# A TensorE bank lent for one decay, the attention norm by tokens, and a shifted split between VectorE and GpSimd in a state-space and attention kernel

## The chip, the cores and the metric

One core of one Trainium2 chip runs the whole kernel. The metric is the time of one execution on the device in microseconds (us). The page and the trace show one profiled execution; the times of the table come from runs of their own. Engines: PE is TensorE (PEld its weight loads), DVE VectorE, ACT ScalarE, POOL GpSimd, SP the engine on whose queue all DMAs of the loop are issued.

## The reference, cut to what matters

The input x is (8, 96, 64, 64): eight batches, 96 channels, 4096 positions ("tokens"). Everything is fp32 but the last block.

```python
# layer 0: group norm, then a selective state-space block
xz = u @ in_proj_w.T;  xm, z = halves of 192 channels
xm = silu(causal depthwise conv of 4 taps(xm) + conv_b)
dt, Bm, Cm = xm @ x_proj_w.T          # 6, 16, 16 columns
delta = softplus(dt @ dt_proj_w.T + dt_proj_b)
h_t = exp(delta_t * A) * h_(t-1) + delta_t * B_t * u_t   # 192 channels x 16 states
y_t = C_t . h_t + D * u_t
out = layernorm_c((y * silu(z)) @ out_proj_w.T) * gamma + beta
x = x + out
# layer 1: linear attention (no softmax) of 6 heads on t = tokens of x
t = t + ((q k^T / 4) v) @ Wff + bff    with q, k, v from layernorm(t) @ Wqkv + bqkv
# then a feed-forward 96 -> 384 -> 96 in 8-bit products on layernorm(t)
t = t + ffn(layernorm(t))
```

Since the attention has no softmax, it needs of a batch only the 97x97 Gram matrix of the normed tokens with a row of ones ("G" below): four small products ("fold") turn G into a matrix that is applied to every token.

## The kernel before, in words

**Tiling.** A batch is cut into 8 chunks of T = 512 positions; 64 chunks are worked one after the other. The states of a chunk are laid out as 24 blocks of 128 rows, 6 "quads" (s) of 4 blocks (q): quads 0 to 3 hold the lower 128 channels (LOWS), quads 4 and 5 the upper 64 (HIGHS).

**Per block.** ACT computes the decay exp(delta*A) of a block into one of two PSUM banks DA (decay, L834); DVE scans it, h = decay*h + D, into R (scan, L1271). D, the product of delta*u and B, has room for three quads: DVE forms it for quads 0 and 1 and for the first SPLIT = 240 columns of quad 3 (inputs, L1255; its B stands in the PSUM bank PB, copied there by ACT: put_b, L820), POOL for quads 2, 4 and 5 (inputs, L648) and the rest of quad 3 (rest, L657). POOL also multiplies R by C, one instruction per quad (product, L669), and forms delta*u (delta_u, L641). PE sums the products over the states (sum_states, L1639 and L1643) into the bank Y, and DVE gates them with silu(z) (gate, L1292).

**Around it.** In iteration g the block work is that of chunk g. PE and ACT prepare chunk g+1 (silu L782 to L789 with a table load before and after, x_proj, state_rows L796, dt_proj, softplus) and g+2 (norm L773, conv L1596 and L1599, z_proj). They finish chunk g-1 (out_proj, square L840, variance, inv_ln L845, inv_std L849, scale_out L1296, add_x, keep_x1 L882, centre) and the attention's part of g-2: DVE's token_norm (L1304) makes th, the normed x1; PE transposes it (to_tokens L1700), ACT copies it to tT (token_copy L877), PE forms four products of 128 tokens (gram L1709) and DVE adds them to G (L1330). Chunks g-10 to g-12, a batch later, go through attention and the feed-forward (centre_tokens L1751, variance_x2, inv_ln_x2 L892, norm_x2 L1351, up, hidden L901, down, output L923, x2 sums, result L916).

**Order.** Every engine has one queue with its order written out by hand in its function iteration(g). Waits are on semaphores; the names Progress hold a count per chunk. The four general PSUM banks G0 to G3 pass from use to use, each guarded by what last read it (freed in PE's iteration). SP's queue is one order too: a DMA that waits holds all behind it. B, C, delta and delta*u are spread over the 128 rows through DRAM: spill writes them, spread_delta, spread_du, load_b and load_c read them back (L487, L489, L509, L515). keep_th (L440) stores th.

## Time and profile before

| | |
|---|---|
| median of 3 runs | 2515.29 us (2514.42 to 2517.96) |
| profiled execution | 2515.68 us, its span 2513.9 us |
| mean granted TensorE clock in it | 0.986 |
| DVE, POOL, ACT, PE busy | 98%, 96%, 92%, 85% of the span |
| DMA | 494.54 MB, mean 197 GB/s |

The span runs from the first instruction to the last; 1.8 us lie around it. A busy share is that of the whole span, with its start (60 us) and its end (some 100 us), in which other work is done than in the loop. Busy time counts an instruction from its start to its end; neighbours on one engine overlap by 0.05 to 0.1 us, so that the distance of two starts is what an instruction costs.

### The profile page before, as it was taken

What the parts mean: (1) busy time and instruction counts of PE and PEld (TensorE: products, weight loads), DVE (VectorE), ACT (ScalarE), POOL (GpSimd) and SP (SyncE); (2) the same over time, 40 slices, a digit from 0 to 9 for tenths busy, and PEclk for the clock granted to TensorE, in tenths of its full rate; (3) what the DMA queues carried; (4) which work ended last, traced back from release to release, by engine and by line L of the source; (5) the groups of instructions that cost most, each with busy time, mean ns of one, the idle gap of its engine ahead of it and who ended that gap; (6) DMA issues with size and microseconds to landing.
All of it is one profiled execution on the core that took longest, in us unless ns stands there. A gap on an engine that the chain in (4) does not pass through costs nothing.

```text
span 2513.9 us, 35083 instructions
## 1 busy us (share of the span) xinstructions
PE 2145.8 (85%) x10314; PEld 827.2 (33%) x10314; DVE 2456.3 (98%) x2391; ACT 2316.1 (92%) x3960; POOL 2418.5 (96%) x719
## 2 busy tenths in 40 slices
PE   6888888888888888888888888888888888888878
PEld 3334434333323323323333323323323333333323
DVE  6999999999999999999999999999999999999986
ACT  5777777999999999999999999999999999999977
POOL 4999999999999999999999999999999999999991
PEclk8899999999999999999999999999999999999979
DMA  6555555656656656656656666566566565566542
GB/s 240 192 184 167 199 185 175 210 197 199 217 197 205 211 198 205 210 203 203 207 203 206 204 207 209 198 209 210 196 210 209 197 209 201 189 211 199 183 141 75
DMA packets 171388, 494.54 MB, mean 197 GB/s; under 512 B 23072, under 2 KB 44704, under 8 KB 154240
## 3 DMA queue, kind: packets, MB, share of 16 engines
q1 hardware_dynamic: 171200, 492.30, 58.2%
q8 instruction: 85, 1.39, 0.2%
q14 instruction: 103, 0.84, 0.1%
HBM read 400.33 MB, written 91.88 MB: 196 GB/s over the span
## 4 chain that ended last, share of the span: by engine, by line
DVE 66%; POOL 14%; issue 12%; PE 3%; ACT 3%; DMA 0%; DVEq 0%; POOLq 0%; ACTq 0%; SPq 0%
DVE R L1271 50%; POOL R L669 10%; DVE D L1255 10%; POOL D L648 3%; DVE q L1351 1%; ACT DA L834 1%; DVE dl L1281 1%; DVE G L1296 1%; DVE yv L1292 1%; PE G L1562 1%; POOL D L657 1%; DVE th L1304 1%; POOL du L641 1%; PE Y L1643 1%; PE Y L1562 0%
## 5 line engine op out<-in xcount | busy, mean ns | idle before, releaser
L1271 DVE TENSOR_TENSOR_SCAN R<-DA,R,D 128x512 f32<-128x512 f32 x1344 | 1633.6, 1270 | 1.0 <-ACT DA L834 1.0
L669 POOL TENSOR_TENSOR R<-R,Cs 128x2048 f32<-128x2048 f32 x383 | 1453.8, 3821 | 0.0
L834 ACT ACTIVATE DA<-ds,kept_w 128x512 f32<-128x512 f32 x1536 | 1054.9, 688 | 143.4 <-DVE R L1271 129.4
L648 POOL TENSOR_TENSOR D<-us,Bs 128x2048 f32<-128x2048 f32 x193 | 738.0, 3824 | 9.8 <-DMA us<-lo_d 9.8
L1255 DVE TENSOR_TENSOR D<-us,PB 128x2048 f32<-128x2048 f32 x191 | 360.3, 1886 | 7.2 <-DMA us<-lo_d 7.2
L1596 PE MATMUL G<-un,wcv 96*128 96x512 f32 x512 | 251.7, 614 | 29.4 <-ACT h L901 29.4
L1639 PE MATMUL Y<-R,kept_w 128*32 128x512 f32 x2048 | 265.3, 613 | 8.3 <-POOL R L669 8.3
L1271 DVE TENSOR_TENSOR_SCAN R<-DA,D 128x512 f32<-128x512 f32 x192 | 221.9, 1206 | 2.1 <-ACT DA L834 2.1
L1599 PE MATMUL G<-un,wcv 96*64 96x256 f32 x1024 | 138.9, 393 | 60.5 <-ACT xq L882 59.2
L1562 PE MATMUL G<-st,kept_w 128*64 128x256 f32 (+1 forms) x384 | 108.9, 485 | 54.3 <-ACT st L796 54.3
L1596 PEld LDWEIGHTS G<-un,wcv 96*128 96x128 f32 x512 | 87.9, 189 | 187.8 <-issue 113.8
L1562 PE MATMUL G<-sq,kept_w 96*96 96x512 f32 (+1 forms) x256 | 136.7, 616 | 13.2 <-DVE dl L1281 12.6
L1643 PE MATMUL Y<-R,kept_w 128*32 128x256 f32 x2048 | 138.1, 388 | 7.7 <-POOL R L669 7.6
L657 POOL TENSOR_TENSOR D<-us,Bs 128x1088 f32<-128x1088 f32 x64 | 135.7, 2121 | 4.4 <-DVE R L1271 4.0
L1562 PE MATMUL G<-q,w1q 96*128 96x512 fp8e5 x164 | 63.1, 388 | 77.7 <-DVE q L1351 45.4
L905 ACT ACTIVATE h<-h,b1q 128x512 f16<-128x512 f16 x165 | 117.2, 711 | 0.0
L1599 PEld LDWEIGHTS G<-un,wcv 96*64 96x64 f32 x1024 | 62.6, 136 | 148.3 <-ACT xq L882 111.3
L1562 PE MATMUL G<-un,kept_w 96*64 96x256 f32 x372 | 108.1, 470 | 0.0
L1639 PEld LDWEIGHTS Y<-R,kept_w 128*32 128x32 f32 x2048 | 47.6, 110 | 162.3 <-issue 106.3
L641 POOL TENSOR_TENSOR du<-dl,u 128x768 f32<-128x768 f32 x63 | 97.9, 1554 | 0.0
L820 ACT COPY PB<-Bs 128x512 f32<-128x512 f32 x191 | 95.6, 500 | 0.0
L901 ACT CAST h<-G 128x512 f16<-128x512 f32 x164 | 94.8, 578 | 0.3 <-PE G L1562 0.3
(239 smaller groups left out, 3348.6 us busy)
## 6 DMA issues: line engine op xcount, KB each, us to landing
Bs<-bc_d SPq DMA_DIRECT2D x128, 512.0 KB, 5.7
us<-lo_d SPq DMA_DIRECT2D x64, 1024.0 KB, 6.6
ds<-lo_d SPq DMA_DIRECT2D x64, 1024.0 KB, 8.7
Cs<-bc_d SPq DMA_DIRECT2D x128, 512.0 KB, 4.8
us<-hi_d SPq DMA_DIRECT2D x64, 512.0 KB, 7.0
ds<-hi_d SPq DMA_DIRECT2D x64, 512.0 KB, 5.4
lo_d<-dl SPq DMA_DIRECT2D x64, 256.0 KB, 2.0
lo_d<-du SPq DMA_DIRECT2D x64, 256.0 KB, 2.0
```

The lines of the kernel that those rows point to most:

```text
L641: nc.gpsimd.tensor_tensor(du[:, :], dl[:, :], u[:, place(k) % 2, :], ALU.mult)\
L648: nc.gpsimd.tensor_tensor(shaped(D[:, s % NDBU, :, :], s), low(us, s) if s in LOWS else high(us), of_states(Bs, s), ALU.mult).then_inc(don ...
L657: nc.gpsimd.tensor_tensor(D[:, s % NDBU, :, cs], us[:, 0:QUAD, cs], Bs[:, h, w, cs].unsqueeze(1).to_broadcast([128, QUAD, T - SPLIT[s]]), ...
L669: nc.gpsimd.tensor_tensor(shaped(R[:, s, :, 0:T], s), shaped(R[:, s, :, 1:S], s), of_states(Cs, s), ALU.mult).then_inc(hc_done.sem, 1)
L834: nc.scalar.activation(DA[j % NDA][:, :], ds[:, i, :], ACT.Exp, scale=A[:, j:j + 1]).then_inc(exp_done.sem, 1)
L1255: nc.vector.tensor_tensor(D[:, s % NDBU, :, 0:n], us[:, 0:QUAD, 0:n], PB[:, 0:n].unsqueeze(1).to_broadcast([128, QUAD, n]), ALU.mult)\
L1271: nc.vector.tensor_tensor_scan(R[:, s, q, 1:S], DA[j % NDA][:, :], D[:, s % NDBU, q, :], before, ALU.mult, ALU.add).then_inc(scanned.sem, 1)
L1562: return mm(o, left, right, start=True, stop=True)
L1596: last = mm(o[:, :], wcv[:, t, 0:LOW], un[:, t:t + T], start=(t == 0), stop=(t == TAPS - 1))
L1599: last = mm(o[rows, 0:H], wcv[:, t, LOW:LOW + HIGH], un[:, t + cs.start:t + cs.stop], start=(t == 0), stop=(t == TAPS - 1))
L1639: last = mm(Y[32 * q:32 * q + 32, :], sumsel, R[:, s, q, 0:T], start=s == 0, stop=s == 3)
L1643: last = mm(Y[at:at + 32, 0:H], sumsel, R[:, s, q, cs], start=False, stop=s == 5 and q > 1)
```

## The change

All but the first three points are in the layer-1 work of chunks g-1 and g-2 or follow from it.

- **Split.** SPLIT of quad 3 goes from 240 to 304: DVE forms 64 columns more of that quad's D (four rows of them), POOL 64 fewer.
- **Lent bank.** The decay of block (1, 0) goes into G0, not into a DA bank. PE's lend signals that G0 is free (after token_scale of chunk g-2 has read it); ACT's decays (0,3) and (1,0) stand ahead of silu then. From block (1,2) on the two DA banks alternate as before.
- **B of quad 1 by PE.** A 0/1 matrix (state_row) picks B's rows out of st and PE writes them into PB; ACT's copy of 512 columns goes. ACT still puts B for quads 0 and 3.
- **Attention norm by tokens.** PE centres x1 in four products that come out with tokens on the rows (centre_by_token); the channel form of the centring stays, for the squares, and the second variance is formed by token, four products of one column (variance_by_token). ACT's second Ln and Exp work on 128x4 values (token_ln, token_std), four ACT instructions of 96 columns scale the centred tokens into tT (token_scale), PE transposes them back (from_tokens) and ACT copies th (th_copy). DVE's token_norm and ACT's 128x384 token_copy go.
- **Gram sum by PE.** PE adds the old G with an identity product ahead of the four products; ACT copies the sum to G (gram_copy), DVE's addition goes.
- **Eps row.** The variance's constant comes in through a 97th row of avg and a row of ones in sq and fsq, so that Ln has no bias operand.
- **Orders.** On POOL product 1 goes ahead of inputs 4 and product 2 ahead of inputs 5. DVE's, ACT's and PE's orders and the banks are changed throughout. SP's order stays, but keep_th waits for th_copy.

```diff
-FRONT = (3, 1, 4, 2)
+FRONT = (3, 1, 2, 4)
-SPLIT = {3: 240}
+SPLIT = {3: 304}
+BORROWS = 4
...
 # POOL's iteration
                     product(g, 0)
+                    product(g, 1)
                     inputs(g, 4)
                 if there(g + 1):
                     delta_u(g + 1)
                 if there(g):
-                    product(g, 1)
+                    product(g, 2)
                     inputs(g, 5)
-                    product(g, 2)
                     product(g, 3)
                     product(g, 4)
...
 # ACT
+            def decay(k, s, q, borrowed=None):
                 j = QUAD * s + q
...
+                if borrowed is not None:
+                    act.wait_ge(lent.sem, lent.at(k))
+                elif j - NDA == BORROWS:
+                    act.wait_ge(scanned.sem, scanned.at(k, j + 1 - 2 * NDA))
+                else:
+                    act.wait_ge(scanned.sem, scanned.at(k, j + 1 - NDA))
+                to = DA[j % NDA] if borrowed is None else borrowed
...
-                nc.scalar.activation(rs[:, :], src[0:C, :], ACT.Ln, bias=epsn[0:C, :]).then_inc(post_ln.sem, 1)
+                nc.scalar.activation(rs[:, :], src[0:C, :], ACT.Ln).then_inc(post_ln.sem, 1)
...
+            def token_ln(k, src):
+                act.wait_ge(tok_mm.sem, tok_mm.at(k, 2))
+                act.wait_ge(post_act.sem, post_act.at(k - 1, 5))
+                nc.scalar.activation(rsT[:, :], src[:, 4 * C:4 * C + T // 128], ACT.Ln).then_inc(post_ln.sem, 1)
+            def token_scale(k, src):
+                act.wait_ge(post_act.sem, post_act.at(k, 4))
+                act.wait_ge(post_mm.sem, post_mm.at(k - 1))
+                act.wait_ge(th_mm.sem, th_mm.at(k - 1))
+                for a in range(T // 128):
+                    last = nc.scalar.activation(tT[:, a, 0:C], src[:, a * C:(a + 1) * C], ACT.Identity, scale=rsT[:, a:a + 1])
+                last.then_inc(post_act.sem, 1)
+            def th_copy(k, src):
+                act.wait_ge(th_mm.sem, th_mm.at(k))
+                if there(k - 1):
+                    act.wait_ge(th_out, kept(k - 1))
+                nc.scalar.copy(th[0:C, :], src[0:C, :]).then_inc(th_done.sem, 1)
+            def gram_copy(k, src):
+                act.wait_ge(post_mm.sem, post_mm.at(k))
+                nc.scalar.copy(G[:, :], src[0:C + 1, 0:C + 1]).then_inc(g_done.sem, 1)
...
 # start of ACT's iteration, new: token_std(g-2), decay(0,1), token_scale(g-2), decay(0,2), decay(0,3),
 # decay(1,0,G0), silu(g+1), decay(1,1), decay(1,2), gram_copy(g-2), th_copy(g-2), decay(1,3),
 # state_rows(g+1), decay(2,0), result(g-12), decay(2,1), output(g-11), put_b(g,3), decay(2,2), ...
 # its end: ... decay(5,2), hidden(g-10,2), put_b(g+1,0), hidden_bias x2, decay(5,3), hidden_round(g-10),
 # decay(g+1,0,0), token_ln(g-1,G0)
...
 # DVE's iteration, new: scan(0,0), scan(0,1), gate(g-1,0), scan(0,2), scan(0,3), inputs(g,1), gate(g-1,1),
 # scan(1,0,G0), scan(1,1..3), scan(2,0..2), inputs(g,3), scan(2,3), delta(g+1), scale_out(g-1), scan(3,0..3),
 # scan(4,0), norm_x2(g-10), scan(4,1..3), scan(5,0..2), inputs(g+1,0), scan(5,3)
...
 # PE
+            def put_b(k, s):
+                if k == 0 and s == 1:
+                    return
+                pe.wait_ge(st_done.sem, st_done.at(k))
+                pe.wait_ge(dbu_d.sem, dbu_d.at(k, BY_DVE[s] - steps_to(k, s)))
+                one(PB[:, :], state_row[32:64, (1,).index(s), :], st[32:64, :]).then_inc(b_put.sem, 1)
...
+            def centre_by_token(k, o):
+                pe.wait_ge(x1_done.sem, x1_done.at(k))
+                for a in range(T // 128):
+                    last = one(o[:, a * C:(a + 1) * C], x1[:, a * 128:(a + 1) * 128], cen)
+                last.then_inc(tok_mm.sem, 1)
+            def variance_by_token(k, o):
+                pe.wait_ge(post_act.sem, post_act.at(k, 3))
+                for a in range(T // 128):
+                    last = one(o[:, 4 * C + a:4 * C + a + 1], sq[:, a * 128:(a + 1) * 128], avg[:, 0:1])
+                last.then_inc(tok_mm.sem, 1)
+            def from_tokens(k, o):
+                pe.wait_ge(post_act.sem, post_act.at(k, 5))
+                for a in range(T // 128):
+                    last = nc.tensor.transpose(o[0:C, a * 128:(a + 1) * 128], tT[:, a, 0:C], eye)
+                last.then_inc(th_mm.sem, 1)
...
             def gram(k, o):
...
+                if add:
+                    pe.wait_ge(g_done.sem, g_done.at(k - 1))
+                    mm(o[0:C + 1, 0:C + 1], eye[0:C + 1, 0:C + 1], G[:, :], start=True, stop=False)
...
 # start of PE's iteration, new: wait for token_scale(g-2) (or what else last used G0), lend(g), put_b(g,1),
 # add_skip(g-1,1), sum_states(g-1,4), sum_states(g-1,5), x_proj(g+1,G1), gram(g-2,G2), wait for scan(1,0),
 # from_tokens(g-2,G0), x2_tokens(g-12,G3), ..., down(g-11,G1), wait for th_copy(g-2), out_proj(g-1,G0),
 # dt_proj(g+1,0,G3), dt_proj(g+1,1,G1), variance(g-1,G2), sum_states(g,0), centre_tokens(g-10,G2), ...
 # its end: ... up x3, variance_by_token(g-1,G0), sum_states(g,2), conv and z_proj of g+2, sum_states(g,3)
```

## Rows read from the trace of the kernel before

**Rows 1.** The page's first part: busy us, share of the span, number of instructions.
```profile
PE 2145.8 (85%) x10314; PEld 827.2 (33%) x10314; DVE 2456.3 (98%) x2391; ACT 2316.1 (92%) x3960; POOL 2418.5 (96%) x719
```
**Rows 2.** By stretches: its length, busy us (instructions) per engine, clock, DMA.
```profile
core 0: us, PE busy (x) PEld busy (x) DVE busy (x) ACT busy (x) POOL busy (x), PEclk, DMA share, GB/s
960.00:1260.00 300.00, 258.14 (x1254) 95.92 (x1254) 299.70 (x285) 294.86 (x513) 299.63 (x88) 1.00 0.61 205
```
**Rows 3.** Waits: POOL's of the run, ACT's from 600 to 2100; us, times, longest.
```profile
POOL D L657 <- DVE R L1271: 4.0, 8, 1.4
...
ACT DA L834 <- DVE R L1271: 19.2, 44, 0.5
```
**Rows 4.** DVE in order of time: start, length, line; and the gates' group (mean ns).
```profile
1204.97 0.68 DVE L1304 TENSOR_TENSOR th<-G,rs 96x512 f32<-96x512 f32 x1
1205.57 1.27 DVE L1271 TENSOR_TENSOR_SCAN R<-DA,R,D 128x512 f32<-128x512 f32 x1
1206.76 2.26 DVE L1255 TENSOR_TENSOR D<-us,PB 128x2048 f32<-128x2048 f32 x1
...
1215.17 0.23 DVE L1330 TENSOR_TENSOR G<-G 97x97 f32<-97x97 f32 x1
...
1220.96 1.13 DVE L1255 TENSOR_TENSOR D<-us,PB 128x960 f32<-128x960 f32 x1
...
1229.14 7.15 DVE L1271 TENSOR_TENSOR_SCAN R<-DA,R,D 128x512 f32<-128x512 f32 x6
...
L1292 DVE TENSOR_TENSOR yv<-Y,z 128x512 f32<-128x512 f32 (+1 forms) x128 | 69.1, 540 | 11.1 <-PE Y L1643 10.0 <-PE Y L1639 0.4
```
**Rows 5.** POOL: two groups of the run (busy, mean ns), then rows in time.
```profile
L648 POOL TENSOR_TENSOR D<-us,Bs 128x2048 f32<-128x2048 f32 x193 | 738.0, 3824 | 9.8 <-DMA us<-lo_d 9.8
L657 POOL TENSOR_TENSOR D<-us,Bs 128x1088 f32<-128x1088 f32 x64 | 135.7, 2121 | 4.4 <-DVE R L1271 4.0
...
80.44 3.82 POOL L648 TENSOR_TENSOR D<-us,Bs 128x2048 f32<-128x2048 f32 x1
...
1221.43 1.54 POOL L641 TENSOR_TENSOR du<-dl,u 128x768 f32<-128x768 f32 x1
...
1226.71 3.81 POOL L648 TENSOR_TENSOR D<-us,Bs 128x2048 f32<-128x2048 f32 x1
...
2410.36 3.81 POOL L648 TENSOR_TENSOR D<-us,Bs 128x2048 f32<-128x2048 f32 x1
```
**Rows 6.** ACT: rows in time, then groups of the run (busy, mean ns).
```profile
1205.22 1.28 ACT L782 ACT_TABLE_LOAD   x1
...
1209.64 1.37 ACT L834 ACTIVATE DA<-ds,kept_w 128x512 f32<-128x512 f32 x2
1210.94 0.57 ACT L916 COPY xt<-G 96x512 f32<-96x512 f32 x1
1211.42 0.47 ACT L877 COPY tT<-G 128x384 f32<-128x384 f32 x1
...
L845 ACT ACTIVATE rs<-G,epsn 96x512 f32<-96x512 f32 x126 | 85.1, 675 | 1.7 <-PE G L1562 1.7
L840 ACT ACTIVATE sq<-G 96x512 f32<-96x512 f32 x126 | 73.0, 580 | 0.4 <-PE G L1660 0.4
L744 ACT ACTIVATE gt<-PB,epsn 96x1 f32<-96x1 f32 x7 | 1.8, 252 | 0.0
```
**Rows 7.** PE in time: the Gram's products, one chunk; then a pair for variance.
```profile
1212.75 0.85 PE L1709 MATMUL G<-tT 128*97 128x97 f32 x8
...
1219.91 1.10 PE L1562 MATMUL G<-sq,kept_w 96*96 96x512 f32 x2 [0.23 <-DVE dl L1281]
```
**Rows 8.** SP in time; then DMA issues: count, KB each, median us to landing.
```profile
1225.99 0.55 SPq L487 DMA_DIRECT2D us<-lo_d  x1
...
us<-lo_d SPq DMA_DIRECT2D x64, 1024.0 KB, 6.6
ds<-lo_d SPq DMA_DIRECT2D x64, 1024.0 KB, 8.7
```

More of the change, by code:

```diff
@@ L950, in iteration @@
                 if place(g + 3) == 0 and later(g + 3):
-                    group_square(g + 3, PB, 2)
+                    group_square(g + 3, PB, 1)
                 if there(g):
                     decay(g, 1, 2)
-                if there(g + 1):
-                    state_rows(g + 1, G3)
+                if place(g + 3) == 0 and later(g + 3):
+                    group_square(g + 3, PB, 2)
+                if there(g - 2):
+                    gram_copy(g - 2, G2)
+                    th_copy(g - 2, G0)
@@ L956, in iteration @@
                 if there(g):
                     decay(g, 1, 3)
+                if there(g + 1):
+                    state_rows(g + 1, G1)
+                if there(g):
+                    decay(g, 2, 0)
+                if inside(g - 12):
+                    result(g - 12, G3)
+                if there(g):
+                    decay(g, 2, 1)
+                if place(g + 3) == 0 and later(g + 3):
+                    group_scale(g + 3, PB, 1)
                 if inside(g - 11):
                     output(g - 11, G1)
-                if place(g + 3) == 0 and later(g + 3):
-                    group_scale(g + 3, PB, 1)
@@ L986, in iteration @@
                 if there(g - 1):
-                    inv_std(g - 1, 0)
-                if inside(g - 10):
-                    inv_ln_x2(g - 10, G0)
+                    inv_std(g - 1)
+                if place(g + 3) == 0 and later(g + 3):
+                    group_scale(g + 3, PB, 3)
+                if there(g):
+                    decay(g, 3, 1)
                 if ahead(g + 11):
                     chunk_mean(g + 11)
+                if inside(g - 10):
+                    square_x2(g - 10, G2)
+                if ahead(g + 11):
+                    chunk_dev(g + 11)
                 if there(g):
-                    decay(g, 3, 1)
+                    decay(g, 3, 2)
+                if there(g - 1):
+                    keep_x1(g - 1, G0)
+                if there(g):
+                    decay(g, 3, 3)
+                if inside(g - 10):
+                    inv_ln_x2(g - 10, G1)
+                if there(g):
+                    decay(g, 4, 0)
+                if inside(g - 11):
+                    output_bias(g - 11)
                 if inside(g - 10):
@@ L1708, in gram @@
                         pe.wait_ge(last_tokens, 1 + a // 2)
-                    last = mm(o[0:C + 1, 0:C + 1], tT[:, a, :], tT[:, a, :], start=(a == 0), stop=(a == T // 128 - 1))
+                    last = mm(o[0:C + 1, 0:C + 1], tT[:, a, :], tT[:, a, :], start=(a == 0 and not add),
+                              stop=(a == T // 128 - 1))
                 last.then_inc(post_mm.sem, 1)
@@ L1823, in iteration @@
                     group_centre(g + 3, PB)
-                if there(g + 1):
-                    if g == 0:
-                        freed(dl_done, 0)
-                    x_proj(g + 1, G3)
+                if there(g - 2):
+                    freed(silued, g + 1, 3)
+                    gram(g - 2, G2)
+                    freed(scanned, g, 5)
+                    from_tokens(g - 2, G0)
+                if 0 < g < 12:
+                    freed(silued, g + 1)
+                    spin(2, G3, *weights)
@@ new lines, in iteration @@
+                if inside(g - 12):
+                    freed(silued, g + 1)
+                    x2_tokens(g - 12, G3)
+                if place(g + 3) == 0 and later(g + 3):
+                    group_var(g + 3, PB)
+                if 0 < g < 12:
+                    spin(2, G3, *weights)
+                if inside(g - 12):
+                    x2_plain(g - 12, G3)
+                if 0 < g < 12:
+                    spin(1, G3, *weights)
+                if inside(g - 12):
+                    x2_feed(g - 12, G3)
@@ new lines, in iteration @@
+                if there(g + 1):
+                    (freed(f_out, g - 12) or freed(silued, g + 1))
+                    dt_proj(g + 1, 0, G3)
+                    (freed(f_y16, g - 11) or freed(st_done, g + 1))
+                    dt_proj(g + 1, 1, G1)
+                if there(g - 1):
+                    ((place(g - 10) == 0 and freed(fold_ev, g - 10, 4)) or freed(g_done, g - 2)
+                     or freed(silued, g + 1, 3))
+                    variance(g - 1, G2)
+                if there(g):
+                    sum_states(g, 0)
@@ L2136 @@
     chans, states = np.stack(chans, 1), np.stack(states, 1)
+    state_row = np.zeros((64, 1, 128))
+    for i, s in enumerate((1,)):
+        state_row[32 + 8 * LOWS[s][0] + 2 * (row % NSUB) + LOWS[s][1], i, row] = 1.0
     avg = np.full((C, C), 1.0 / C)
```

440 lines of the change are left out of this document (197 added, 243 removed).

## The prediction

> **What bounds the kernel now.** I read the page's busy shares first: DVE 98%, POOL 96%, ACT 92%, PE 85% [rows 1]. Such an average does not tell which of three full engines sets the pace, so the table by stretches came next. In the middle of the run DVE is busy 299.70 us of 300, POOL 299.63, ACT 294.86, PE 258.14 [rows 2]. The waits say the same: POOL waits for DVE 4.0 us in the whole run, and in the 1500 us from 600 to 2100 ACT waits 19.2 us, for scans [rows 3]. The loop's period is read on POOL, which does the same eleven instructions per chunk: its first product D of chunk 1 starts at 80.44, that of chunk 63 at 2410.36 [rows 5], so 62 periods of 37.58 us. POOL's own work is 9 instructions of 2048 elements (3.82 us each, L669's products like L648's), the piece L657 2.12 and du 1.54 [rows 5], each less the 0.05 that it shares with its neighbour: 9 x 3.77 + 2.07 + 1.50 = 37.5. So POOL is the pace from 80 us on, DVE stands within 0.1 us of it, and ACT with 19.2/40 = 0.48 us of waiting per chunk works 37.0. All three must get lighter for the period to fall; one alone gives nothing.
>
> **POOL, split 304.** L657 goes from 272 to 208 columns of four rows, 1088 to 832 elements. From 3824 ns for 2048 and 2121 for 1088 [rows 5] one element costs 1.774 ns; 256 fewer save 0.45 us per chunk. New POOL work: 37.1. Bounds: by proportion to 2121 ns, 0.50; and nothing less than 0.40, since both rows are steady in every chunk. Taken 0.45.
>
> **DVE.** Removed: the attention norm L1304, which starts at 1204.97 and lets the next scan start at 1205.57, so 0.60; the Gram sum, 0.23 less the 0.08 by which neighbours overlap, 0.15. Added: 256 elements of L1255. 2048 elements take 2.26 us and 960 take 1.13 [rows 4], 1.04 ns each, so 0.27. Net -0.48 us per chunk: DVE work 37.46 (its 299.70 over eight chunks of 37.5) becomes 37.0.
>
> **ACT.** Instructions overlap their neighbour by about 0.1 us (a 0.57 us row is followed after 0.48, a 0.47 row after 0.37) [rows 6]. Removed per chunk: B of quad 1, a copy of 512 columns like the one at 1210.94, 0.48; the second Ln, 0.68 less 0.1; the second Exp, without a bias operand and so as the Square L840, 0.48; the token copy 0.37: 1.91. Added: the copy th 0.48; the Gram copy of 97 columns, a quarter of the 384-column row at the least (0.12), taken 0.15; B of quad 3 longer by 64 columns, 0.05; Ln and Exp of 4 columns, 0.1 to 0.2 each; four scalings of 96 columns. The scalings are not in the trace: below, a quarter of the 384-column copy each, 0.37 in all; above, four rows like L744 (0.25, a PSUM source with a bias from SBUF) with 0.08 for the columns, less 0.1 overlap, 0.92. They keep each instruction's fixed part, so I take 0.9. The eps row takes the bias operand from two remaining Ln: the row with it has 675 ns, the Square without it 580 on the same shape, so -0.19 for both. Sum: 0.48 + 0.15 + 0.05 + 0.3 + 0.9 - 0.19 - 1.91 = -0.2 us, bounds -0.8 and 0. ACT work 36.8, below POOL's 37.1, with 0.3 to spare.
>
> A rule prices the same scalings: the Trainium skill ("ScalarE: Activation LUTs", section "What ACT_TABLE_LOAD costs") gives an ACTIVATE a fixed part of 186 ns plus 0.833 ns per element, 93 ns more for each pointer operand, and an overlap of 93 ns. By it a 96-column scaling with one pointer is 0.27 us, four 1.06, and ACT comes out near 0 rather than at -0.2. The 95 ns between the Ln and the Square rows agree with its 93. Here the rule speaks a little against the change, and would leave ACT at 37.0, still under POOL.
>
> **PE.** The pair that forms one 96x512 product takes 1.10 us, the eight that form the Gram's four products 0.85 [rows 7]. Added: B of quad 1 at 1.1; the sum's identity product 0.2; four centrings by token 0.85; four variances of one column, between nothing and 0.85, taken 0.7 since their weights are loaded all the same; longer transposes 0.1. Removed: one variance, 1.1. Net +1.8 of the 5.2 us that PE idles per chunk (300 - 258.14 over eight), so no bound by sum. What counts is order. PB by PE waits for the third split product of the chunk before (inputs(g,0)) and for the token scaling that frees G0; behind it stand add_skip and the sums of quads 4 and 5, for which gate(g-1,1) waits. That gate now has four scans and a product ahead of it, so it waits later than before; I cost it nothing. If this cover is gone, the price is the lateness itself.
>
> **The lent bank.** It lets ACT put a third decay (G0) ahead of the two table loads and four Silu, a block of 4.4 us (1205.22 to 1209.64) [rows 6]. DVE shows no wait there now, so it gives nothing by itself; it covers DVE's loss of the norm as filler. G0's way back is narrow: from_tokens may write G0 only after scan(1,0), and th_copy after it stands in ACT's queue ahead of decay(1,3). Counting from scan(0,0): five scans at 1.19, the product 2.18 and the two gates (0.54 each by their row, less overlap) end near 9.0, the transposes near 9.7, th_copy 10.3, decay(1,3) 11.0, and scan(1,3) wants it two scans after 9.0, at 11.3. Margin 0.3 us.
>
> **POOL's new order.** product 1 goes ahead of inputs 4, product 2 ahead of inputs 5. inputs(g,5) ended at 1230.5 (1226.71 + 3.8) [rows 5] and scan(5,0), the fifth of the six from 1229.14 [rows 4], started at 1233.9: 3.4 to spare. It moves 3.77 later, gets 0.45 back, and DVE arrives 0.48 earlier: -0.4. So DVE waits here until it stands that much behind POOL, then no more. The loop POOL (product 5, inputs 2, rest, products 0 and 1, inputs 4, du, product 2, inputs 5: 29.5) then DVE (four scans and a product, 6.9) with two handovers is about 36.6, under 37.1: half a microsecond of play, no new bound. du moves 3.3 later too, and with it on SP's queue the spill of du, load_b(g+1,0), the us load and the ds load behind it. us was issued at 1225.99 and lands after 6.6 [rows 8], 3.6 us before inputs(g+1,0) at 1236.2 (which is 1229.14 and six scans). The product is moved behind one more scan (+1.18) and comes 0.48 earlier; with POOL's phase 0.15 nearer about 1.1 us is left. keep_th waits for th_copy, near 10.3 instead of 2.5, and holds back SP's ds high, xt, tn, xq and Cs loads; their users are centre_tokens (which moved behind sum_states(g,0), near 15) and product 2 (near 22). Nothing of it is late by more than PE's slack.
>
> **Start and end.** Two memsets of one partition stand on DVE ahead of the first statistics, and the kept weights grow by 256 columns, 131 KB, which at the 205 GB/s of rows 2 is 0.6 us. Both lie in the first 40 us, beside loads that DVE and POOL wait for: between nothing and 1.5, taken 0.5. The tail after the last scan loses one norm and gains four scalings beside it: nothing, 1 either way.
>
> **Sum.** The profiled execution took 2515.68 us, 0.4 over the median 2515.29 of the runs. 63 chunks x 0.45 = 28, plus 0.5 for the start: 2515.7 - 28.4 + 0.5 = 2487.8, and 2487.4 from the median: 2488.
>
> **Rivals.** *Half the gain (chance 0.20).* us lands late for inputs(g+1,0). That is a loop: POOL from product 5 to du (five products or inputs, the piece, du: 22.0), the spill up to the us issue (du ends at 1222.97, issue 1225.99: 3.0), the landing, inputs 2.2, a scan 1.2, handovers 0.2: 28.6 plus the landing. At 6.6 it is 35.2 and idle; at the 8.7 that the load of the same size, ds, takes in the median [rows 8] it is 37.3: 62 x 0.28 = 17 saved, so 2498. For it: du moves later; against it: the loads about us (Bs before, ds behind) stay the same in the same order. *Nothing (0.07).* The scalings and handovers cost ACT 0.8 more than taken; ACT's period is 37.6, the time 2515. *Slower (0.13).* ACT waits for PE at the Gram copy and th_copy. Behind Silu the way is u, x_proj (as long as two of the 1.1 pairs, 2.0), the Gram with its identity product (1.05), transposes 0.6, th_copy, while ACT has only z, a table load and two decays between: it arrives about when PE is done, so any lateness of PE (the sums of quad 5 ahead of x_proj wait for product 5) is ACT's. ACT has 36.8 of work: a wait of 0.3 is free, 0.8 eats the whole gain, and above that the kernel is slower; at 1.2 the period is 38.0, 62 x 0.42 = 26 more, 2541. For it: ACT has the least idle time of its own and stands in order; against it: its waits today are all for scans [rows 3], and PE has 3.4 us of idle left.
>
> The forecast has 0.60. Range: 2479 (POOL at 0.50 per chunk and the small waits gone) to 2518; its own range alone is 2482 to 2494. With 0.2% (5 us) as what a measurement tells from none: faster 0.80, same 0.07, slower 0.13.
>
> **What would show it.** L657 at about 1.67 us; L1255 at 1216 elements near 1.4; POOL's starts 37.1 apart with no wait; DVE with a few tenths of waiting per chunk before scan(5,0) for POOL; ACT waiting 0.3 to 0.6 us per chunk. Wrong would be: POOL idle by over 0.3 us per chunk, ACT waiting for PE behind the Silu block by over 0.3, a wait for us, or scalings above 0.3 each.

## The result and the profile after

| | before | after |
|---|---|---|
| median of 6 runs | 2514.93 us (2514.42 to 2517.96) | 2587.6 us (2565.42 to 2619.5) |
| after / before | | 1.025 [1.0233, 1.0268] |
| profiled execution, its span | 2515.68, 2513.9 | 2582.9, 2580.9 |
| mean granted TensorE clock | 0.986 | 0.926 |
| mean period of a chunk | 37.56 | 38.58 |

The forecast was 2488, with 2479 to 2518 as range. The kernel is slower by 73 us and lies outside. The ratios in this text leave out runs over 1.5% above the fastest of their kernel (two of this kernel's six, two of e3's five and one of e12's six), so this kernel's ratio is below the quotient of the medians, 1.029. Periods in this text are distances of the starts of POOL's du, as means over the 61 chunks from du(2) to du(63), du(k) being that of chunk k. "Falls" are the stretches at half the granted clock, counted from 120 us, behind the start, to du(63).

The page of the kernel after, its first part (beside [rows 1]) and the clock line of its second, 40 equal slices of the span, in tenths:

```profile
PE 2384.5 (92%) x11432; PEld 1021.1 (40%) x11432; DVE 2438.7 (94%) x2268; ACT 2297.9 (89%) x4211; POOL 2393.2 (93%) x719
...
PEclk8899999998879999998989998989989899899988
```

DVE, ACT and POOL are busy for less time than before, by 18, 18 and 25 us, though the span grew by 67. PE's busy time grew by 239, more than twice the 1.8 x 62 = 112 of the forecast. The same by stretches, beside [rows 2]: length, busy us per engine, the clock, DMA.

```profile
core 0: us, PE busy (x) PEld busy (x) DVE busy (x) ACT busy (x) POOL busy (x), PEclk, DMA share, GB/s
660.00:960.00 300.00, 283.87 (x1306) 115.96 (x1304) 280.62 (x255) 275.76 (x514) 279.08 (x84) 0.90 0.58 195
960.00:1260.00 300.00, 280.64 (x1365) 117.45 (x1363) 292.30 (x266) 287.86 (x536) 291.07 (x87) 0.94 0.60 200
1002.00:1003.00 1.00, 0.00 (x0) 0.00 (x0) 1.00 (x2) 1.00 (x5) 1.00 (x1) 1.00 0.75 246
1004.00:1005.00 1.00, 1.00 (x11) 0.36 (x14) 1.00 (x2) 0.98 (x3) 1.00 (x2) 1.00 0.78 273
1005.00:1006.00 1.00, 1.00 (x16) 0.58 (x12) 1.00 (x2) 1.00 (x1) 1.00 (x1) 0.51 0.22 80
1008.00:1009.00 1.00, 1.00 (x6) 0.63 (x3) 1.00 (x3) 1.00 (x1) 1.00 (x2) 0.78 0.00 0
1180.00:1190.00 10.00, 9.91 (x39) 4.05 (x38) 10.00 (x8) 10.00 (x17) 9.58 (x3) 0.63 0.85 314
1190.00:1200.00 10.00, 10.00 (x43) 3.29 (x45) 5.51 (x6) 5.84 (x14) 7.60 (x2) 0.69 0.26 87
```

No engine is full in the first two rows, and the clock that was 1.00 in [rows 2] is 0.90 and 0.94. The one-microsecond rows show what such a mean is made of: 1.00 up to 1005, then 0.50 for 3.4 us, up to the middle of the 1008 row. So TensorE alternates between 2.4 and 1.2 GHz. The last two rows lie in a longer fall: PE is busy all the time, while DVE has only 5.51 us of work in ten and POOL 7.60. A page that rounds to tenths hides this as a row of 8s and 9s; [rows 2] gave the number to hold it against.

Waits of after from 600 to 2100 (in all, times, longest), beside [rows 3]:

```profile
POOL R L676 <- DVE R L1314: 48.0, 48, 3.2
...
DVE yv L1335 <- PE Y L1677: 42.8, 10, 5.2
...
POOL D L664 <- DVE R L1314: 21.8, 9, 3.5
ACT u L789 <- PE Y L1691: 21.1, 10, 2.7
```

DVE waits for PE ten times for 4.3 us each, POOL then for DVE, and ACT for PE. The waits for PE are few and long, not a few tenths in each of the 39 chunks. POOL's starts of du say which chunks pay:

```profile
321.99 1.55 POOL L648 TENSOR_TENSOR du<-dl,u 128x768 f32<-128x768 f32 x1
...
359.12 1.56 POOL L648 TENSOR_TENSOR du<-dl,u 128x768 f32<-128x768 f32 x1
...
396.20 1.56 POOL L648 TENSOR_TENSOR du<-dl,u 128x768 f32<-128x768 f32 x1
...
1172.95 1.54 POOL L648 TENSOR_TENSOR du<-dl,u 128x768 f32<-128x768 f32 x1
...
1214.95 1.55 POOL L648 TENSOR_TENSOR du<-dl,u 128x768 f32<-128x768 f32 x1
```

The early chunks take 37.13 and 37.08, the forecast's 37.1; they test POOL alone, since the attention's and feed-forward's work for DVE and ACT is not in them yet. The one at 1172.95, with the long fall, takes 42.0. There are 49 falls, 307 us in all: 37 of 3.4 us and 12 of 13.7 to 23.9 us. They begin at two places of a chunk only: 32 at 8 to 11 us behind the start of du (place B, all the long ones among them), 17 at 19 to 22 us (place A). No chunk has two. The 12 chunks with a long fall are together 59 us longer than at 37.29 each, the period of e5 below. PE in order of time, at A (first rows) and at B (from 1178.76 on, where the first row is the last of the centring's eight rows):

```profile
1000.31 1.06 PE L1677 MATMUL Y<-R,kept_w 128*32 128x512 f32 x8
1001.31 0.65 PE L1593 MATMUL G<-un,kept_w 96*64 96x256 f32 x4
1003.15 1.09 PE L1593 MATMUL PB<-st,kept_w 32*128 32x512 f32 x2 [1.18 <-ACT tT L883]
1004.17 0.65 PE L1691 MATMUL Y<-u,kept_w 64*64 64x256 f32 x4
1004.75 3.43 PE L1681 MATMUL Y<-R,kept_w 128*32 128x256 f32 x32
...
1178.76 0.28 PE L1593 MATMUL G<-kept_w,xq 96*128 96x96 f32 x1
1179.84 0.59 PE L1593 MATMUL G<-q,w1q 96*128 96x512 fp8e5 x2 [0.80 <-issue]
1180.52 1.05 PE L1593 MATMUL G<-kept_w,sq 97*128 97x1 f32 x8
1181.50 1.06 PE L1677 MATMUL Y<-R,kept_w 128*32 128x512 f32 x8
1182.49 1.98 PE L1630 MATMUL G<-un,wcv 96*64 96x256 f32 x8
...
1184.80 3.62 PE L1627 MATMUL G<-un,wcv 96*128 96x512 f32 x4
...
1195.68 1.28 PE L1677 MATMUL Y<-R,kept_w 128*32 128x512 f32 x8
```

At A PE waits 1.18 us for ACT's token_scale ahead of put_b, and then does narrow work: 32 rows of weights for B, 64 by 64 for add_skip, 32-column sums. The fall covers nearly all of the sums: 3.43 us, where the same rows take 1.93 at full clock. At B stand the centring by token (96 columns each), 0.80 us without an instruction, and the variance by token (one column each): its eight rows start 0.11 us apart and leave PE busy by the profile, though each has one column to work on. Behind them eight products take 1.98 in place of 1.08 and four 3.62 in place of 1.88 (rows of a chunk at full clock). The sum of quad 3 ends at 1197.0, by the full-clock rows of the same groups some 6 us late, and DVE, which gates with it, starts its yv at 1197.04 after 4.49 us of waiting.

The kernel before has none of this at the chunk's start. PE of before, in order of time, between the gate and the sums of quads 4 and 5:

```profile
1167.26 0.65 PE L1653 MATMUL Y<-u,kept_w 64*64 64x256 f32 x4 [1.02 <-DVE yv L1292]
1167.86 1.10 PE L1769 MATMUL G<-tn,MT 97*96 97x512 f32 x2
1168.89 1.07 PE L1643 MATMUL Y<-R,kept_w 128*32 128x256 f32 x16
1169.89 1.10 PE L1761 MATMUL G<-xt,kept_w 96*96 96x512 f32 x2
```

It idles as long (1.02 us), but two pairs of wide products, of 97 and 96 rows by 512 columns, stand between the narrow ones, and the clock stays at 1.00 there [rows 2]. The change moved those products behind x_proj. That this is what keeps the clock was not tested by itself.

### The profile page after: what moved, and what is told of

Same layout as the page of the kernel before. It is cut to its first block, busy times and chain, and to the rows that moved or that the text cites. A ratio compares the mean times of both kernels' runs of the same rounds, so it can differ in the third digit from the quotient of the medians.

```text
span 2580.9 us, 37582 instructions
## 1 busy us (share of the span) xinstructions
PE 2384.5 (92%) x11432; PEld 1021.1 (40%) x11432; DVE 2438.7 (94%) x2268; ACT 2297.9 (89%) x4211; POOL 2393.2 (93%) x719
## 4 chain that ended last, share of the span: by engine, by line
POOL 25%; issue 18%; ACT 13%; PE 13%; DVE 9%; DMA 4%; SPq 2%; POOLq 0%; ACTq 0%; DVEq 0%
POOL R L676 13%; POOL D L655 9%; DVE R L1314 5%; ACT DA L849 5%; DMA xg<-in_x 3%; PE G L1593 2%; PE G L1627 2%; DVE D L1297 2%; PE Y L1681 2%; PE G L1630 1%; POOL D L664 1%; POOL du L648 1%; PE Y L1677 1%; ACT h L944 1%; ACT h L951 1%
## 5 line engine op out<-in xcount | busy, mean ns | idle before, releaser
L1314 DVE TENSOR_TENSOR_SCAN R<-DA,R,D 128x512 f32<-128x512 f32 x1288 | 1556.6, 1263 | 22.6 <-ACT DA L849 19.5
L849 ACT ACTIVATE DA<-ds,kept_w 128x512 f32<-128x512 f32 x1472 | 1000.5, 685 | 119.4 <-DVE R L1314 89.8
L1677 PE MATMUL Y<-R,kept_w 128*32 128x512 f32 x2048 | 297.1, 654 | 10.8 <-POOL R L676 10.8
L1627 PE MATMUL G<-un,wcv 96*128 96x512 f32 x512 | 284.9, 686 | 0.0
L1630 PE MATMUL G<-un,wcv 96*64 96x256 f32 x1024 | 177.9, 480 | 0.0
L664 POOL TENSOR_TENSOR D<-us,Bs 128x832 f32<-128x832 f32 x64 | 106.7, 1667 | 27.3 <-DVE R L1314 27.3
L1335 DVE TENSOR_TENSOR yv<-Y,z 128x512 f32<-128x512 f32 (+1 forms) x128 | 69.6, 544 | 60.3 <-PE Y L1677 55.2
L1593 PE MATMUL G<-un,kept_w 96*128 96x512 f32 x372 | 123.2, 522 | 0.0
L1677 PEld LDWEIGHTS Y<-R,kept_w 128*32 128x32 f32 x2048 | 41.2, 110 | 167.9 <-issue 111.2
L1593 PE MATMUL PB<-st,kept_w 32*128 32x512 f32 x126 | 71.0, 643 | 34.7 <-ACT tT L883 34.3
L1681 PEld LDWEIGHTS Y<-R,kept_w 128*32 128x32 f32 x2048 | 68.1, 125 | 76.2 <-issue 43.1
```

The costliest lines, as they stand in the source:

```text
L664: nc.gpsimd.tensor_tensor(D[:, s % NDBU, :, cs], us[:, 0:QUAD, cs], Bs[:, h, w, cs].unsqueeze(1).to_broadcast([128, QUAD, T - SPLIT[s]]), ...
L849: nc.scalar.activation(to[:, :], ds[:, i, :], ACT.Exp, scale=A[:, j:j + 1]).then_inc(exp_done.sem, 1)
L1314: nc.vector.tensor_tensor_scan(R[:, s, q, 1:S], by[:, :], D[:, s % NDBU, q, :], before, ALU.mult, ALU.add).then_inc(scanned.sem, 1)
L1593: return mm(o, left, right, start=True, stop=True)
L1627: last = mm(o[:, :], wcv[:, t, 0:LOW], un[:, t:t + T], start=(t == 0), stop=(t == TAPS - 1))
L1630: last = mm(o[rows, 0:H], wcv[:, t, LOW:LOW + HIGH], un[:, t + cs.start:t + cs.stop], start=(t == 0), stop=(t == TAPS - 1))
```

## The experiments

"Both" below means the first two edits together. For each kernel: median, ratio to before with its interval, period, falls in the 61 chunks and their sum.

| kernel | median us | ratio | period | falls | us at half clock |
|---|---|---|---|---|---|
| before | 2515 to 2516 | | 37.56 | 0 | 0 |
| after | 2587.6 | 1.025 [1.0233, 1.0268] | 38.58 | 32 B, 17 A | 307 |
| e1_wide | 2551.28 | 1.015 [1.0131, 1.0169] | 37.93 | 44 (12 B, 31 A) | 188 |
| e2_early | 2580.55 | 1.024 [1.0185, 1.0296] | 38.60 | 16 B, 33 A | 307 |
| e3_both | 2553.15 | 1.0094 [1.0054, 1.0133] | 37.72 | 6 B, 30 A | 143 |
| e4_split | 2525.51 | 1.0037 [1.0024, 1.0051] | 37.71 | 2 | 10 |
| e5_fill | 2504.84 | 0.9964 [0.9951, 0.9977] | 37.29 | 0 | 0 |
| e6_fill2 | 2503.91 | 0.9962 [0.9949, 0.9975] | 37.31 | 0 | 0 |
| e7_act_b | 2599.94 | 1.031 [1.0251, 1.0368] | 39.06 | 31 B, 22 A | 389 |
| e8_no_spin | 2529.39 | 1.0059 [1.0044, 1.0074] | 37.78 | 13, early | 92 |
| e9_fill_a | 2551.91 | 1.0148 [1.013, 1.0167] | 38.00 | 25 (24 B) | 150 |
| e10_fill_b | 2519.35 | 1.0011 [1.0003, 1.002] | 37.58 | 25 A | 92 |
| e11_mean_late | 2612.97 | 1.0386 [1.0351, 1.0421] | 39.42 | 24 B | 273 |
| e12_best | 2620.79 | 1.0402 [1.0373, 1.0431] | 39.08 | 19 B | 218 |
| e13_stats_early | 2502.19 | 0.9945 [0.9932, 0.9957] | 37.23 | 2 | 7 |
| e14_mean_late_3 | 2530.94 | 1.0063 [1.0048, 1.0079] | 37.75 | 1 | 3 |

Period and falls go by the one profiled execution, which is the shortest of its kernel's runs for e1, e3 and e9 and the longest for e7 and e11. In kernels whose clock falls they can be off by a good deal, and the medians weigh more.

**e1_wide: the variance by token 32 columns wide.**

```diff
-                nc.scalar.activation(rsT[:, :], src[:, 4 * C:4 * C + T // 128], ACT.Ln).then_inc(post_ln.sem, 1)
+                nc.scalar.activation(rsT[:, :], src[:, 4 * C:4 * C + 128].rearrange("p (a c) -> p a c", c=32)[:, :, 0], ACT.Ln).then_inc(post_ln.sem, 1)
...
-                    last = one(o[:, 4 * C + a:4 * C + a + 1], sq[:, a * 128:(a + 1) * 128], avg[:, 0:1])
+                    last = one(o[:, 4 * C + 32 * a:4 * C + 32 * a + 32], sq[:, a * 128:(a + 1) * 128], avg[:, 0:32])
```

> The changed kernel with one edit: each of the four variance products by token writes 32 equal columns (the averaging matrix's first 32) instead of one; Ln reads every 32nd. The values are the same. Theory A (clock): TensorE's granted clock falls to half behind the stretch centre_by_token, up, variance_by_token, in which its products are 96 and 1 columns wide, because the engine does too little there; with 32 columns that place fills up. Expected: the falls that begin at the sum of quad 2 (8 to 9 us after du starts) go or become rare, those at the sums of quads 4 and 5 stay; time 2510 to 2565. Theory B (order): PE is late at full clock because it has 1.8 us more per chunk, and the falls come behind the waits without causing them; nothing changes here: 2565 to 2590, as many falls as before.

The falls at B went from 32 to 12 and the time by 36 us (all of its runs, 2543 to 2561, are below all of after's), while those at A went from 17 to 31: that these would stay as they were was wrong. The products with 32 columns take as long as those with one (1.08 us for the eight rows, 1.05 in after), so next to nothing but their width changed at B.

**e2_early: put_b(g,1) ahead of the wait for token_scale.**

```diff
                 if there(g):
+                    put_b(g, 1)
...
                     lend(g)
-                    put_b(g, 1)
```

> The changed kernel with one edit: PE's put_b(g,1) stands ahead of the wait for token_scale and of lend(g), instead of behind them, so that the 1.2 us in which PE stood idle at the start of a chunk hold the product of 1.1 us. Theory A (clock): the falls that begin at the sums of quads 4 and 5 (about 20 us after du starts) go, those behind the one-column products stay; time 2520 to 2580. Theory B (order): PE gains its 1.1 us once per chunk, so the time falls whatever the clock does, to about 2515 to 2540, with the falls unchanged in number.

The time did not move beyond its scatter, and Theory A's expectation failed: the falls at A did not go but went from 17 to 33, and those at B, which the edit does not touch, from 32 to 16. After has 49 falls and e2 has 49, one in a chunk: where one place is spared, the other is hit. So the falls of one place do not tell what an edit is worth. The wait went where it could: put_b follows at once, and PE then waits at add_skip for DVE's gate (26 times between 600 and 2100, 1.1 us in the mean), with the same narrow work behind it. Moving an idle stretch is not removing it.

**e3_both: the two edits together.**

> The changed kernel with both edits, 32-column variance products and put_b(g,1) ahead of lend. Theory A (clock): few falls are left between 100 us and the last chunk; chunks take 37.1 us by POOL's starts, as the undisturbed ones of the changed kernel do (37.06 to 37.16), and the time is 2488 to 2500. Theory B (order): chunks still take 37.5 or more without a fall, the time is above 2515.

The falls at B are rare now, those at A stay: 30 in 61 chunks. Theory A missed, with few falls and 2488 to 2500. Theory B's time, above 2515, was met, but not its reason, that chunks take 37.5 or more without a fall: of those without one some take 37.06. The five runs reach from 2528.69 to 2576.76; their median is 1.015 of before's.

**e4_split: before, with SPLIT = {3: 304} alone.**

> The kernel before with SPLIT 304 instead of 240 and nothing else. If DVE and POOL were both the pace, POOL gets 0.45 us per chunk lighter and DVE 0.27 heavier: DVE's 37.46 becomes 37.7, POOL waits for scans by some 0.6 per chunk, and the time rises by about 62 x 0.2 = 12 us to 2520 to 2530. If POOL alone were the pace and DVE had room, the time would fall to about 2490.

DVE's work of 37.46 plus 0.27 for 256 elements makes 37.73; measured 37.71. DVE alone sets the pace when it is the heavier. That the two numbers meet is in part luck: the mean holds the early chunks, six of which (in chunks 3 to 9) take 37.06 to 37.21 since DVE has less to do there. Between du(15) and du(55) the period is 37.79 and DVE is busy all of it, where it is busy 37.53 per chunk in the kernel before: the 0.27 holds (0.26), the 37.46 was 0.07 low. The early chunks show POOL's new load, near 37.1.

**e5_fill: both, and fillers at A and at B.** A filler is a product whose result nobody reads.

```diff
                 pe.wait_ge(dbu_d.sem, dbu_d.at(k, BY_DVE[s] - steps_to(k, s)))
+                spin(2, PB, *weights)
                 one(PB[:, :], state_row[32:64, (1,).index(s), :], st[32:64, :]).then_inc(b_put.sem, 1)
...
+                    spin(1, G1, *weights)
                     up(g - 10, 0, G1)
```

> The changed kernel with 32-column variance products, put_b(g,1) ahead of lend, and filler products whose result nobody reads: two of 128x128 by 256 columns into PB ahead of put_b's product (where PE else waits 1 us for the gate), one into G1 ahead of up(g-10,0) (where PE else waits 0.5 us). Theory A (clock): with the two weak places filled the granted clock stays at 1 in the loop; chunks take 37.1 to 37.3 us and the time is 2488 to 2505, though PE does 1.2 us more per chunk. Theory B (order, PE too full): 1.2 us more of PE work makes every chunk later, 2550 to 2600.

No fall in any chunk, 48 us less than e3 and 83 less than after: 2504.84, faster than before by 0.36%. PE got three products more per chunk (128 by 128 by 256; from the first's start to the next product's, the two at A take 1.06 us and the one at B 0.69). The stretch of before's [rows 2] in it, and two waits from 600 to 2100:

```profile
960.00:1260.00 300.00, 286.07 (x1457) 123.87 (x1456) 299.11 (x273) 295.33 (x550) 299.20 (x90) 1.00 0.62 207
```

```profile
ACT xg L728 <- DMA xg<-in_x: 14.2, 24, 2.1
...
POOL R L676 <- DVE R L1314: 10.2, 24, 2.0
```

DVE and POOL are at 299 of 300 again, the waits of DVE and ACT for PE are gone but for 0.5 us. PE is busier than in the stretches of after, so its sum was never the bound.

**e6_fill2: two fillers at B.**

> As the run with fillers, with two filler products ahead of up(g-10,0) instead of one, 0.4 us more than the idle time there. Theory A: falls behind the variance by token go altogether; if the filler is free of cost the time is the same as with one, within 5 us; if PE has become the pace it is 0.2 to 0.4 us per chunk longer, 12 to 25 us. Theory B: longer by 25 us or more.

The same time; one filler is enough there, and 0.4 us more of PE costs nothing.

**e7_act_b: after, with B of quad 1 put by ACT again.**

```diff
+                if there(g):
+                    put_b(g, 1)
                 if there(g - 2):
                     token_std(g - 2)
...
                     lend(g)
-                    put_b(g, 1)
```

> The changed kernel with B of quad 1 put into PB by ACT's copy of 512 columns again, at the start of ACT's chunk, and not by PE. PE is lighter by 1.1 us per chunk, ACT heavier by 0.48, at 37.2 to 37.3 by its sum. Theory A (clock): the place at the chunk's start gets emptier, since 1.1 us of products go and the wait stays: at least as many falls there; the falls behind the one-column products stay too; time 2560 to 2600. Theory B (PE too full): PE has 1.1 us back, the time falls to 2510 to 2530, set by ACT.

PE has 1.1 us less to do per chunk, and there is no gain in time; its runs reach from 2577 to 2616. Its profile, of the longest of them, has four falls more than after's and 82 us more at half clock. The rival by which PE has too much work, and which gave 2510 to 2530, is out.

**e8_no_spin: before, without its own fillers.** The kernel before has 15 fillers per chunk in PE's iterations 1 to 11, in the places where the attention's and feed-forward's products stand later.

```diff
-                    spin(2, G0, *weights)
+                    spin(0, G0, *weights)
...
```

> The kernel before without the filler products in PE's iterations 1 to 11, where the second layer's work is still missing; nothing else is changed. Theory A (clock): between 40 and 480 us the granted clock falls in most chunks, as in the changed kernel, and later, where no filler is ever issued, it stays at 1; the chunks concerned take 0 to 5 us longer each, the time is 2520 to 2560. Theory B: fillers only cost or do nothing, the time is 2512 to 2517.

By stretches, e8_no_spin and then before:

```profile
100.00:400.00 300.00, 242.70 (x1090) 86.86 (x1088) 285.91 (x263) 222.28 (x366) 290.74 (x86) 0.85 0.54 180
500.00:800.00 300.00, 258.28 (x1254) 95.83 (x1250) 299.58 (x284) 294.10 (x509) 299.70 (x89) 1.00 0.60 204
```

```profile
100.00:400.00 300.00, 265.10 (x1360) 122.21 (x1356) 295.41 (x274) 229.92 (x378) 300.00 (x89) 0.99 0.54 184
```

Where the fillers are gone the clock is 0.85 and most chunks take 38.1 to 40.6; behind that stretch all is as before. The clock costs the kernel before the same thing, from the other side. It fits with after's chunks 2 to 9, which take 37.06 to 37.19: there its own fillers stand. Two falls at A, of 3.4 us, are in them all the same, in chunks of 37.06 and 37.16: a short fall can cost nothing.

**e9_fill_a and e10_fill_b: both, with the fillers of one place each.**

> The changed kernel with 32-column variance products, put_b(g,1) ahead of lend, and the two fillers into PB ahead of put_b's product, but none ahead of up(g-10,0). Theory A (clock, each weak place by itself): the falls 19 to 22 us after du's start, 30 of 36 in the profile without fillers, are gone; the few 9 to 11 us after it stay, with the long ones (13.7 us) among them; time 2505 to 2530. Rival (only the sum of PE's idle time counts, wherever it is): both kinds fall alike.

> As before it, with the one filler ahead of up(g-10,0) and none into PB. Theory A: the falls 9 to 11 us after du's start are gone, those 19 to 22 us after it stay; they are 3.4 us long each and cost 0.2 to 0.5 us per chunk; time 2508 to 2525. Rival: both kinds fall alike.

By stretches, a fall at B of e9_fill_a, and one at A of e10_fill_b:

```profile
785.00:793.00 8.00, 8.00 (x23) 2.60 (x23) 7.47 (x6) 7.07 (x13) 8.00 (x3) 0.50 0.93 369
793.00:802.00 9.00, 9.00 (x23) 2.83 (x22) 3.89 (x4) 6.18 (x13) 8.41 (x3) 0.51 0.25 78
```

```profile
569.00:570.00 1.00, 0.96 (x12) 0.48 (x16) 1.00 (x1) 0.98 (x3) 1.00 (x2) 0.97 0.62 221
570.00:571.00 1.00, 1.00 (x16) 0.43 (x8) 1.00 (x2) 1.00 (x1) 1.00 (x1) 0.50 0.03 8
```

With e3 and e5 they are the four cases of two switches. Each filler removes the falls of its own place, all of them. That at B leaves those at A about as they were (30 and 25); that at A brings more at B, 24 where e3 has 6, and the time stays where it was: e9's expectation, that the few falls at B would stay and the time be 2505 to 2530, missed. The rival, by which both kinds fall alike, missed too. By the ratios the filler at B is worth 0.8% where A has none (e3 to e10; 1.3% by the medians) and 1.8% where it has (e9 to e5); that at A is worth 0.5% where B has one (e10 to e5) and shows nothing where it has none (e3 to e9), under the scatter of the long falls. The place whose falls can be long is the costly one.

**e11_mean_late: e5_fill, with ACT's mean and deviation of a later chunk moved back.** To meet the wait for xg that e5 still shows.

```diff
-                if ahead(g + 11):
-                    chunk_mean(g + 11)
                 if inside(g - 10):
                     square_x2(g - 10, G2)
-                if ahead(g + 11):
-                    chunk_dev(g + 11)
...
                     keep_x1(g - 1, G0)
+                if ahead(g + 11):
+                    chunk_mean(g + 11)
                 if there(g):
                     decay(g, 3, 3)
+                if ahead(g + 11):
+                    chunk_dev(g + 11)
```

> The kernel with both fillers, and on ACT chunk_mean one decay later (behind keep_x1) and chunk_dev behind decay(3,3). In the kernel with fillers ACT waited 14.2 us for the load xg in the 40 chunks from 600 to 2100 us, up to 2.1 at once, which it did not before: that load now stands on SP behind keep_th, and keep_th behind th_copy. If this wait is what lifts the mean period from 37.1 to 37.3, it goes and the period is 37.15: 2504.8 - 62 x 0.15 = 2496. If not, the time stays within 3 us of 2504.

A miss: 108 us slower than e5. Waits from 600 to 2100:

```profile
DVE yv L1335 <- PE Y L1678: 61.7, 13, 5.4
...
PE G L1593 <- DVE q L1388: 36.7, 33, 1.2
```

PE now waits 1.1 us for q ahead of up in 33 of 40 chunks, at place B, with one filler in front, and the clock falls there again: 24 times, for 13.7 to 20.5 us in 14 of them. By which way ACT's new order makes q late was not followed further.

**e12_best: e11_mean_late, and in chunk 0 POOL's product 1 behind du(1).**

```diff
-                    product(g, 1)
+                    if g > 0:
+                        product(g, 1)
...
+                    if g == 0:
+                        product(g, 1)
```

> As the run before it, and POOL does product 1 of chunk 0 behind du of chunk 1, as the kernel before did in all chunks. With the new order du of chunk 1 started at 60.1 us and not at 56.3; the loop begins 3.8 us earlier if du of chunk 1 is what it waits for: 3 to 4 us less than the run before. If POOL is the pace by the sum of its work, the order in chunk 0 moves work and takes none away: no difference above 1 us.

No gain; with the scatter of e11's falls under it, a few microseconds either way could not be seen in the time. The trace tells more: du(1) starts at 60.10 (60.03 in e11), behind 2.01 us in which POOL does nothing. So product 1 ahead of it was not all that held it.

**e13_stats_early: e5_fill, with SP's load of xg ahead of keep_th.**

```diff
+                if ahead(g + 11):
+                    load_stats(g + 11)
                 if there(g - 2):
                     keep_th(g - 2)
...
-                if ahead(g + 11):
-                    load_stats(g + 11)
```

> The kernel with both fillers, ACT's order as in it, and on SP's queue load_stats(g+11) ahead of keep_th(g-2) instead of behind spill_bc(g+1). If ACT's wait for xg (14.2 us in 40 chunks) is the 0.2 us per chunk above 37.1, it goes, POOL's starts come 37.1 to 37.2 apart and the time is 2495 to 2500. If it is covered by other waits, the time stays at 2503 to 2506. PE's order is untouched, so by the clock theory no falls come back.

The fastest kernel of the study: 2502.19, 0.9945 [0.9932, 0.9957] of before. ACT's two longest waits in it from 600 to 2100:

```profile
ACT fsq L926 <- PE G L1811: 3.6, 6, 1.9
ACT DA L849 <- DVE R L1314: 2.9, 8, 0.8
```

The 14.2 us of xg are gone, but only 2.6 us came back, between the two expectations, and its interval overlaps e5's. So little fits with a wait that was mostly ACT's own slack.

**e14_mean_late_3: e11_mean_late with three fillers at B.**

> chunk_mean late on ACT as in the run of 2613 us, with three fillers ahead of up(g-10,0) instead of one. Clock theory: the new order makes norm_x2 late, PE waits longer ahead of the narrow products, and the falls of 13 to 20 us there cost the time; three fillers of 0.4 us each fill the wait, the falls go, the time is 2500 to 2520. Order theory: ACT's new order itself stalls DVE; the time stays above 2580.

One fall is left, and 82 of e11's 108 us are gone. They were the clock's. The time lies between the two expectations, since the other 26 are the order's own: from 600 to 2100,

```profile
DVE R L1314 <- ACT DA L849: 17.7, 47, 0.5
...
ACT fsq L926 <- PE G L1811: 15.3, 39, 1.5
```

ACT comes late with decays at each chunk's middle, which a full clock does not mend.

## Why the prediction was wrong

**POOL, split 304: right.** The row that answers to L657 in [rows 5] is L664, 832 elements in 1667 ns; 1.67 was forecast.

**DVE: right in its terms, 0.1 short in its sum.** 1216 elements take 1394 ns, 1.4 forecast. Between du(15) and du(55) DVE is busy 37.53 us per chunk in before and 37.14 in e5: 0.39 less, 0.48 forecast, from a start that was taken 0.07 low, since 300 us hold 7.98 periods and not eight. So DVE stays level with POOL (37.10 in e5), and the forecast's 37.0 was 0.14 short. The early chunks of after, at 37.06 to 37.19, do not test it.

**ACT: right in its sum and in its largest term.** ACT's groups of after (count, busy us, mean ns, idle before):

```profile
L883 ACT ACTIVATE tT<-G,rsT 128x96 f32<-128x96 f32 x252 | 64.1, 334 | 0.0
...
L890 ACT COPY th<-G 96x512 f32<-96x512 f32 x63 | 36.7, 582 | 11.8 <-PE G L1750 8.4
...
L863 ACT ACTIVATE rs<-G 96x512 f32<-96x512 f32 x63 | 36.3, 576 | 0.7 <-PE G L1593 0.7
...
L917 ACT COPY G<-G 97x97 f32<-97x97 f32 x62 | 14.7, 236 | 16.4 <-PE G L1763 16.4
```

The four scalings start at 1001.83 and the next decay at 1002.72: 0.89 us, 0.9 forecast. Ln went from 675 to 576 ns with its bias operand gone, 0.10 as taken. The waits for PE at the Gram copy and at th are 16.4 and 8.4 us over the run, 0.40 per chunk, over the 0.3 that the prediction named as a sign of being wrong; in e5 they are 1.9 and 1.1 over the run, so they too go with the falls. POOL's idle time, another such sign, is 1.8 us per chunk from 600 to 2100. The Trainium skill ("ScalarE: Activation LUTs", section "What ACT_TABLE_LOAD costs") made the four scalings 1.06; at 0.89 the measurement decides for less by 0.17. Its 93 ns for a pointer agrees with the 99 of the Ln rows.

**PE: the step that failed.** It read "Net +1.8 of the 5.2 us that PE idles per chunk ... so no bound by sum. What counts is order", and costed PE's new order at nothing. The sum was about right: between du(15) and du(55) PE is busy 35.52 us per chunk in e5 and 32.35 in before, and of the 3.2 between them some 1.7 are the fillers; PE still idles. But a free engine was taken as free to idle and to do its products in any order, with each product's duration as a constant from its row. Here durations are not constant. The granted clock, which the page gave as 0.986 and [rows 2] as 1.00, was in the front table and in no term. The change did to it three things at once: it took two wide products from between the narrow ones at the chunk's start, it put a wait for ACT (token_scale) there, and it replaced a 512-column variance by one-column products at B. The term that was put at nothing is (38.58 - 37.29) x 62 = 80 us, with e5 as the kernel without falls (it has the edits of e3 too, and the fillers). The rest of the 99.6 between 2488 and 2587.6, to about 1 us: 0.19 us per chunk above the forecast's 37.1 that e5 has too (DVE's sum and small waits), 12 us; the start and the end, where 0.5 was taken and du(1) starts at 60.05 us in place of 56.32, 4; and 4.7 by which the profiled execution was under its median.

**The lent bank: right as cover, its margin not tested.** No wait for G0's scan shows among the long waits of after; DVE's waits for decays are 5.2 us in 1500 of e5.

**POOL's new order, us and ds: right.** us lands 6.5 and ds 8.8 us after issue in the median, within 0.1 of [rows 8]; DVE's waits for us are 1.1 us in e5. The rival of half the gain is out. keep_th's lateness was named, but xg behind it was not: 14.2 us of ACT's waiting, worth 2.6.

**The rival that ended slower** had its place, PE, but another mechanism: ACT behind the Silu block waiting steadily for PE by over 0.8 us, 2541. Such a wait does show (u for PE's Y, 21.1 us in ten cases), as a result of the falls, and goes with them. Its price was for a small steady wait; the real one is about five microseconds in a chunk in which the clock stays low.

**Was it the clock, or only beside it?** e5, e9, e10 and e3 differ in nothing but products that nobody reads, and the time follows the falls, the long ones above all; e7 takes work from PE and gains nothing; e8 makes falls in the kernel before and loses; e11 and e14 do it once more in another order. What stays open: why a fall at B lasts 3.4 us in 20 cases and 13.7 to 23.9 in 12 (the work behind it is wide, and at half clock PE is busy without a gap); why 12 of the 61 chunks, five of them behind the early ones, have no fall, and why a place that is spared leaves the other more (e1, e2, e9); and which of the three edits brought how many falls, as only the variance was undone by itself.

## What to carry to other kernels

PE had 14% of idle time in the loop and was free by sum, but its idle stretches and its narrow products (here 1, 32, 64 or 96 columns or rows) were a term of their own: ahead of a change that moves them, look at the granted clock by stretches of a microsecond or two around each gap, and count which wide products stand near it. If a profile after a change shows a mean clock lower than before, list where in the loop's period the falls begin, put one or two products that nobody reads at every such place (at one alone, A, they gained nothing here), and only then judge the rest of the change. The change itself, with its clock kept, was worth 0.36%, and 0.55% with SP's order changed too, against the 1.1% forecast.

## What was not expected of the hardware

- More work made the kernel faster: three fillers per chunk took the ratio from 1.0094 [1.0054, 1.0133] (e3) to 0.9964 [0.9951, 0.9977] (e5), and removing fillers from the kernel before cost 14 us.
- The granted clock fell with idle stretches of only 0.7 to 1.2 us in all just before it, and PE busy 1.00 in the row before the fall (1004 to 1005). The Trainium skill ("TensorE: Matmul & The Clock Gate", section "Part 1: The HAM clock gate (the "warmup" mystery)") has two levels, 1.2 and 2.4 GHz, and an idle PE as what leads to the lower; the two levels agree with the rows, but PE's busy share does not tell of the narrow products in it.
- A fall can outlast what began it: 13.7 to 23.9 us at 0.50 while PE's rows follow without a gap. A chunk with one takes 41.0 to 45.3 us, so one costs 4 to 8, and the twelve make 59 of the 80 us.
- Runs of one kernel then scatter by 2% (2565 to 2619), where the kernels without falls keep within 0.2%.
